# One batch projected ahead of layer 0's attention, the other three beneath its first groups

## The reference, cut to what matters

```
x = x + attn0(layernorm(x))      # 16 heads of 8, causal, softmax(q k^T / sqrt(128)) v, then Wo
x = x + moe(layernorm(x))        # 8 experts, top 2, silu(gate) * up, down
x = x + attn1(layernorm(x))      # rms norm, 16 query heads over 4 key heads, no mask, rotary factor
x = x + ffn1(layernorm(x))       # 128 -> 512, a sine transform, relu, 512 -> 128
```

## Time and profile before

| | us |
|---|---|
| median of 3 runs | 1916.95 (1916.47 to 1917.86) |
| profiled execution | 1903.78, its span 1901.6 |
| TensorE busy | 1729.3 |
| VectorE busy | 1371.3 |
| ScalarE busy | 1132.7 |
| GpSimd busy | 307.9 |

### The profile page before, as it was taken

How to read it: one execution, slowest core, us unless ns; L and a number is a source line. 1 busy time by engine, 2 the same in 40 slices (tenths; PEclk the granted TensorE clock), 3 DMA queues, 4 the chain that set the end, 5 groups by cost and what they waited for, 6 DMA issues and landing times.

```text
span 1901.6 us, 30821 instructions
## 1 busy us (share of the span) xinstructions
PE 1729.3 (91%) x10574; PEld 711.1 (37%) x10574; DVE 1371.3 (72%) x2373; ACT 1132.7 (60%) x2396; POOL 307.9 (16%) x407
## 2 busy tenths in 40 slices
PE   4599999998888989999789999999999999999876
PEld 2234444443444346666322222222222222222354
DVE  5577777777778536455787888888888888883386
ACT  2236666665555654333323777777777777777776
POOL 4100000001222225545610000000000000000265
PEclk9779999999999999999656999999999999999998
DMA  7644545333220102131331111111111111000000
GB/s 205 165 95 109 130 127 132 67 46 42 46 41 14 28 23 57 54 90 43 100 77 18 18 18 18 18 18 18 18 18 18 18 18 18 1 2 1 1 23 23
DMA packets 97576, 93.73 MB, mean 49 GB/s; under 512 B 47214, under 2 KB 75507, under 8 KB 95376
## 3 DMA queue, kind: packets, MB, share of 16 engines
q1 hardware_dynamic: 79872, 48.01, 15.3%
q0 software_dynamic: 9920, 37.87, 5.6%
q10 hardware_dynamic: 7632, 5.88, 1.1%
HBM read 48.03 MB, written 40.86 MB: 47 GB/s over the span
## 4 chain that ended last, share of the span: by engine, by line
PE 70%; DVE 14%; ACT 5%; issue 4%; POOL 3%; DMA 3%; ACTq 1%; POOLq 0%; DVEq 0%; SPq 0%
PE ps L855 20%; PE ps L839 17%; PE ps L806 17%; DVE rowmax L1488 8%; PE ps L1035 2%; PE ps L1015 2%; ACT probs L1228 2%; DMA k_parts<-Q 2%; PE ps L1007 2%; PE ps L871 2%; PE ps L1025 2%; ACTq L1145 1%; PE ps L809 1%; PE ps L842 1%; ACT oT L1232 1%
## 5 line engine op out<-in xcount | busy, mean ns | idle before, releaser
L1488 DVE TENSOR_REDUCE rowmax<-ps 128x1 f32<-128x1024 f32 (+7 forms) x1024 | 974.5, 987 | 249.2 <-PE ps L806 125.1
L1228 ACT ACTIVATE probs<-ps 128x512 f32<-128x512 f32 (+3 forms) x1792 | 859.6, 556 | 365.7 <-PE ps L839 225.5
L806 PE MATMUL ps<-K,Q 72*128 72x512 bf16 (+3 forms) x1792 | 541.0, 376 | 41.6 <-DVE rowmax L1488 32.3
L839 PE MATMUL ps<-Q,K 75*128 75x512 bf16 (+3 forms) x1792 | 537.3, 361 | 14.0 <-ACT probs L1228 9.8
L855 PE MATMUL ps<-probs,V 128*9 128x512 f32 (+3 forms) x3584 | 442.2, 555 | 0.0
L839 PEld LDWEIGHTS ps<-Q,K 75*128 75x128 bf16 x1792 | 166.0, 98 | 371.5 <-ACT probs L1228 269.5
L806 PEld LDWEIGHTS ps<-K,Q 72*128 72x128 bf16 x1792 | 151.4, 99 | 338.3 <-DVE rowmax L1488 182.5
L585 POOL TENSOR_SCALAR rtmp<-mv 128x4 f32<-128x4 f32 x8 | 1.9, 234 | 808.3 <-DVE mv L1407 808.3
L809 PE MATMUL ps<-causal,identb 128*128 128x128 bf16 x512 | 115.7, 228 | 0.0
L855 PEld LDWEIGHTS ps<-probs,V 128*9 128x9 f32 x3584 | 60.5, 89 | 144.4 <-ACT probs L1228 77.8
L1736 DVE TENSOR_TENSOR Q<-ps,Q 128x352 f32<-128x352 f32 x78 | 40.9, 524 | 98.5 <-ACT Q L1275 84.6
(11 more groups left out here) (227 smaller groups left out, 1421.5 us busy)
## 6 DMA issues: line engine op xcount, KB each, us to landing
dispatch<-wg POOLq DMA_DIRECT2D x16, 1170.0 KB, 9.0
Q<-q_parts SPq DMA_DIRECT2D x288, 64.0 KB
K<-k_parts SPq DMA_DIRECT2D x144, 64.0 KB
q_parts<-Q POOLq DMA_DIRECT2D x16, 384.0 KB, 3.6
Q<-dispatch SPq DMA_DIRECT2D x78, 65.0 KB, 1.8
probs<-returned SPq DMA_DIRECT2D x8, 512.0 KB, 4.0
k_parts<-Q POOLq DMA_DIRECT2D x8, 384.0 KB, 8.0
V<-v SPq DMA_DIRECT2D x16, 144.0 KB
```

What stands on the lines that cost most here:

```text
L806: last = pe.matmul(buf[:, c:e], Q[0:CROSS, slot, j, i * P:(i + 1) * P], K[0:CROSS, slot, kj, c:e], start=True, stop=not diag)
L839: last = pe.matmul(ps[:, bank, c:HALF], K[0:KROWS, q, kj, t * P:(t + 1) * P], Q[0:KROWS, q, j, h * HALF + c:(h + 1) * HALF], start=True, s ...
L1228: act.activation(probs[:, (4 * m + j) % PR, c:HALF], ps[:, B_BANKS[(4 * m + j) % 3], c:HALF], ACT.Exp, scale=SCALE).then_inc(sl["exp_done" ...
L1488: dve.tensor_reduce(rowmax[:, par, 8 * j + i:8 * j + i + 1], score_a(i % 2)[:, 0:hd.keys(i)], AX, ALU.max).then_inc(sl["max_done"], 1)
```

## The change

Layer 0's `project` now does blocks 0 and 1 only. Blocks 2 to 7 are done by `project_later`, whose steps hang on a events of groups 0 to 4 (`STARTS`), in banks 1 and 3, with their parts in a piece of `attn` that is free until group 8. Statistics are taken batch by batch (`STATS`); POOL inverts batch 0's before its later constants, the others ahead of the blocks' writes. SyncE issues the 20 weight loads instead of ScalarE, behind load(0,1) and ahead of load(0,2), and each `load(b, q)` of layer 0 waits for its own batch's blocks only. In layer 1 `probs` has 16 buffers; the second eight lie in wg and wu, which nothing reads by then. Both strings of `ORDERS` are others. The fills of the dispatch buffers wait for later groups. Of `project_later` there is one on TensorE, ScalarE and VectorE each, in this order below; on ScalarE H copies hT, VT copies V, Q0 and K0 are the high parts (Q0 after the parts of the block before are written), Q1 and K1 the middle ones; on VectorE QR and KR are the rests, Q2 and K2 the low parts.

```diff
-PR = 8
+PR = (8, 16)
 ORDERS = [
-    "bbbbaabpaabbbabapabbbabbpbbbabapcabbbatbpnbababbabbapapaabbababbababbapbbbaabpbampsabbabbabbbappactn",
-    "bbbbababbpbabbapbbababbpbabbabpbbababbpabbapbbababbpbbbapcabbtnbpbabbabbapbabbabbapabbbabpbbbababpmsbbbabapbabbbapapactn",
+    "bbbaabbabapababbabbbappabbababbabbabapbcabbabpbabababtppbnababbabbabbappababbababbabbpbmasbbbappcatn",
+    "bbbbaabbpbabbabbbabbabpbabbabpbababbpbbaabbpbbababpbbababpbabbabpcbababpbabbabpbababbpabbbtpnmsbbbaabbpbabbapbbbaappactn",
 ]
+FIRST = 2
+STARTS = {2: at(1, 0), 3: at(3, 0), 4: at(6, 0), 5: at(9, 0), 6: at(12, 0), 7: at(15, 0)}
+STATS = {1: at(0, 0), 2: at(4, 0), 3: at(10, 0)}
+LATER = {
+    "tensor": steps({}, [("T", at(0, 1)), ("V", at(0, 3)), ("Q", at(1, 1)), ("K", at(1, 1))], STARTS),
+    "scalar": steps({}, [("H", at(0, 2)), ("VT", at(0, 4)), ("Q0", at(1, 2)), ("K0", at(1, 2)), ("Q1", at(1, 4)), ("K1", at(1, 5))],
+                    STARTS),
+    "vector": steps(steps({}, [("SA", 0), ("SB", 2), ("SC", 3)], STATS),
+                    [("N", 0), ("QR", at(1, 2)), ("KR", at(1, 3)), ("Q2", at(1, 5)), ("K2", at(1, 6))], STARTS),
+}
...
                 def load(b, q):
+                    if l == 0:
+                        sp.wait_ge(sl["v_taken"], 2 * b + 2 + AT_ONE)
+                        for half in range(2):
+                            sp.wait_ge(sl["parts_written"][half], 32 * (b + 1))
...
                 for q in range(2):
                     load(0, q)
-                sp.wait_ge(sl["v_taken"], NG + AT_ONE)
-                for half in range(2):
-                    sp.wait_ge(sl["parts_written"][half], 32 * (NG // 2))
+                if l == 0:
+                    for dst, source in weights:
+                        sp.dma_start(dst, source).then_inc(w_in, 16)
+                else:
...
                 load(0, 2)
                 negmax_rows(0, 0)
...
-                    pool.wait_ge(s[0]["attn_done"], (g * fills + c) * 7 // 8 + 1 + AT_ONE)
+                    pool.wait_ge(s[0]["attn_done"], 8 + (g * fills + c) // 2 + AT_ONE)
...
+            def project_later(step):
+                sl = s[0]
+                for kind, u in LATER["tensor"].get(step, ()):
+                    pe.wait_ge(sl["max_done"], 32 + 8 + step - 1)
+                    if kind == "T":
+                        pe.wait_ge(sl["normed"], u + 1)
+                        turn(tokens, 1, sl["turned"])
+                    elif kind == "V":
+                        pe.wait_ge(sl["h_ready"], u + 1)
...
+                    elif kind == "Q":
+                        pe.matmul(ps[:, 1, :], wqvk[:, 0:D], hT[:, :], start=True, stop=True).then_inc(sl["q_out"], 1)
+                    else:
+                        pe.matmul(ps[:, 3, :], wqvk[:, 2 * D:3 * D], hT[:, :], start=True, stop=True).then_inc(sl["k_out"], 1)
...
-            for dst, src in weights:
-                act.dma_start(dst, src).then_inc(w_in, 16)
...
+            def project_later(step):
+                    if kind == "H":
+                        act.wait_ge(sl["turned"], u + 1)
+                        act.activation(hT[:, :], ps[:, 1, :], ACT.Copy).then_inc(sl["h_ready"], 1)
...
+                                if j == 0 and (l == 0 or G * g + m >= PR[1] // 4):
+                                    act.wait_ge(sl["pv_done"], G * g + m + 3 - PR[l] // 4)
...
+            def project_later(step):
+                    if kind[0] == "S":
+                        statistics_of_batch(u, "ABC".index(kind[1]))
+                    elif kind == "N":
+                        dve.wait_ge(sl["rstd_ready"], u // 2 + AT_ONE)
+                        dve.wait_ge(sl["turned"], u)
...
+                    elif kind in ("QR", "KR"):
+                        dve.wait_ge(sl["hi_done"], 2 * u + n + 1)
+                        dve.tensor_tensor(rest_later[:, n, :], ps[:, 1 + 2 * n, :], parts_later[:, n, 0, :], ALU.subtract)\
+                            .then_inc(sl["rest_done"], 1)
+                    else:
+                        dve.wait_ge(sl["mid_done"], 2 * u + n + 1)
...
```

More of the change, by code:

```diff
@@ L514, in _ @@
                     load(0, q)
-                sp.wait_ge(sl["v_taken"], NG + AT_ONE)
-                for half in range(2):
-                    sp.wait_ge(sl["parts_written"][half], 32 * (NG // 2))
+                if l == 0:
+                    for dst, source in weights:
+                        sp.dma_start(dst, source).then_inc(w_in, 16)
+                else:
+                    sp.wait_ge(sl["v_taken"], NG + AT_ONE)
+                    for half in range(2):
+                        sp.wait_ge(sl["parts_written"][half], 32 * (NG // 2))
                 load(0, 2)
@@ L552, in _, with inverse_of_batch @@
             own = Chain(pool, pool_own, own_wait=True)
+            def inverse_of_batch(b):
+                pool.wait_ge(s[0]["stats_ready"], b + 1)
+                apart(pool)
+                tiles = slice(b * BT, (b + 1) * BT)
+                own.done(pool.tensor_scalar(rtmp_b[:, tiles], mv_all[:, tiles, 1], LN_EPS, 1.0, ALU.add, ALU.mult))
+                own.done(pool.tensor_tensor(rstd_all[:, tiles], rtmp_b[:, tiles], power_b[:, :], ALU.pow))
+                pool.sem_inc(rstd_first if b == 0 else s[0]["rstd_ready"], 1)
             own.done(pool.memset(ident[:, :], 0.0))
@@ L565, in _ @@
             pool.wait_ge(consts, 4)
+            inverse_of_batch(0)
+            own.done(pool.memset(ones_rows(0, 2), TWO_ONES))
+            pool.sem_inc(k_ones, 1)
             apart(pool)
@@ L628, in scatter_tile @@
                                         bounds_check=2 * B * S - 1, oob_is_err=False).then_inc(tile_out[k], 16)
-            def inverse_of_batches():
-                for b in range(B):
-                    pool.wait_ge(s[0]["stats_ready"], b + 1)
-                    apart(pool)
-                    tiles = slice(b * BT, (b + 1) * BT)
-                    own.done(pool.tensor_scalar(rtmp_b[:, tiles], mv_all[:, tiles, 1], LN_EPS, 1.0, ALU.add, ALU.mult))
-                    own.done(pool.tensor_tensor(rstd_all[:, tiles], rtmp_b[:, tiles], power_b[:, :], ALU.pow))
-                    pool.sem_inc(rstd_first if b == 0 else s[0]["rstd_ready"], 1)
             def inverse_rms(u):
@@ L778, in project @@
                 projected(0, 0)
+                if l == 0:
+                    projected(1, 1)
+                    return
                 for half in range(2):
@@ L960, in route @@
                     if kind == "WO":
+                        pe.wait_ge(w_in, 16 * len(weights))
                         pe.wait_ge(pre["copied"], TURNS["T1", u] + 1)
@@ L1415, in normalise, with statistics_of_batch @@
                 last.then_inc(done, 1)
-            def project(l):
-                sl = s[l]
-                rows = (P, P if l == 0 else KV * HD)
-                def statistics_of_batch(b):
+            def statistics_of_batch(b, piece):
+                half = BT // 2
+                if piece < 2:
                     dve.wait_ge(x_in[b], 16)
                     apart(dve)
-                    for k in range(BT):
+                    for k in range(piece * half, (piece + 1) * half):
                         last = dve.bn_stats(stats_b[:, k, :], x[:, b * BT + k, :])
                     own.done(last)
+                else:
                     apart(dve)
@@ L1467, in project @@
                 if l == 0:
-                    for b in range(B):
-                        statistics_of_batch(b)
+                    for piece in range(3):
+                        statistics_of_batch(0, piece)
                 norm(0)
@@ L1472, in project @@
                 if l == 0:
-                    dve.wait_ge(sl["rstd_ready"], B - 1 + AT_ONE)
+                    for half in range(2):
+                        body(half, half, False)
+                    return
                 for v in range(NG // 2 - 1):
@@ L1504, in normalise_out @@
                 def normalise_out(g, b, q, h, bank):
+                    if l == 0 and g == 8 and h == 0:
+                        for half in range(2):
+                            dve.wait_ge(sl["parts_written"][half], 32 * (NG // 2))
                     dve.wait_ge(sl["o_turned"], 2 * g + h + 1 + AT_ONE)
```

100 lines of the change are left out of this document (81 added, 19 removed).

## The result

Before: 1917.4 us, median (1916.47 to 1919.89). After: 1955.26 us (1944.46 to 1958.81). The ratio is 1.0192 [1.0168, 1.0216]: the change makes the kernel 37.9 us slower, and the forecast of 1915, with its range to 1935, was wrong. The profiled execution of after took 1958.81 us, 1.8 more than its span.

The account below looks back on a forecast made before the run. Both attentions were taken as bound by TensorE's own instructions. The terms -9.4 + 19.8 + 7.8 + 0.7 + 0.5 - 12 - 9.6 gave -2.2 us, so about 1915 us, range 1896 to 1935.

Parts of the forecast that it names:

- the one for stalls: Groups 0 to 4: stalls from VectorE's waits and added work, 1.3 us a block beside TensorE's 3.3, +7.8 us with statistics apart.
- part 2: Layer 0's attention: six blocks beneath groups 0 to 4, costing +19.8, +7.8, +0.7 and +0.5 us.
- TensorE's work: Groups 0 to 4: six blocks' TensorE instructions all go on the path, 6 x 3.3 = +19.8 us.
- Rival C: Groups 0 to 4: VectorE's wait for ScalarE's high part costs more, whole time 1931 to 1936 us; chance 0.21.
- The start: Ahead of group 0's exponentials: their start moves from 115.9 to about 106.5 us, set by SP's queue, -9.4 us.
- rival B: Ahead of group 0: the weights go beneath the Q and K loads, whole time 1904 us; chance 0.16.
- The orders: Attention groups: new orders save 0.75 us a group in layer 0 (-12) and 0.6 in layer 1 (-9.6).
- Statistics and load(1,0): Groups 0 to 4: three batches' statistics on VectorE +0.7 us; load(1,0) waiting for blocks 2 and 3 +0.5 us.
- the fills': Groups 4 to 7: four dispatch buffer fills a group cost nothing; otherwise the row is late by up to 5 us.

Follow-up runs that it names:

- e5: e4 with TensorE's instructions of the six blocks run a second time in groups 0 to 4, results unread, nobody waiting; 1925.27 us.
- e6: e5 plus ScalarE's copies and VectorE's normalisations, subtractions and statistics of the blocks on their own data, no waits between engines; 1939.27 us.
- e3: The changed kernel with SyncE's weight loads issued behind the first row of negated maxima; 1933.52 us.
- e10: e3 with each block's normalisation four steps earlier on VectorE; 1922.88 us.
- the second one: The kernel before, unchanged, profiled once more; that execution took 1910.74 us.
- e9: e4 with the early start, all eight blocks before attention, own parts buffers, weights on POOL's queue, group 0's row ahead of load(0,2); 1887.75 us.
- e4: The kernel before with both new orders and layer 1's 16 probs buffers, projection and weights as before; 1905.52 us.
- e7: e3 with three windows per block and K taken one window after Q; 1965.81 us.
- e11: The changed kernel with the weights issued by ScalarE on its own queue from 54 us on, instead of SP; 1955.23 us.

## Why the prediction was wrong

**The step that failed** is the one for stalls in part 2: "I take 1.3: +7.8." TensorE's work was right (19.8 forecast, 19.0 in e5). What comes on top of it isn't 7.8 but 33.1 us, 5.5 a block (30.0 by the medians): 14.3 by the other engines' added work and 18.8 by the handoffs, the clock in both. Rival C had the sign and the place, with its threshold of 2.3 us a block; but even its whole price of a routed group, 8.0 a block with TensorE's part, is less than the 8.7 measured. Three things were wrong in the working:

- The lower value was taken because TensorE's own 3.3 us were to "give VectorE time to catch up". e6, where the block's pieces wait for nothing, contradicts it: 14.3 us are lost there all the same.
- The stall was looked for on VectorE, with row maxima behind its wait for ScalarE's high part. In the trace of after waits for row maxima are only 2.2 us, and VectorE itself waits only 1.2 us for high parts. TensorE waits at the block's own instructions, 7.5 us for tokens and 1.5 for hT, and at the next score matmul for a bank that the block used, 5.5 us until VectorE has taken the rests and 2.2 until ScalarE has copied v. TensorE, VectorE and ScalarE, each working in order, meet here several times a block. The routed group from which the bound came has other handoffs.
- The price of a stall was counted as its length. In after against e6 the same instructions took 6.9 us more busy time at the lower granted clock, and in e3 against e10 8.8.

**The start**: -4.1 instead of -9.4 against the forecast's own execution, and +3.0 against the second one; the mechanism was right, the size off, and the gain it was counted on isn't shown to exist. The row landed at 111.6 instead of 106.2. hT came at 16.1, not 14.2, loads at 32.3, not 30.4, so 2 us were late from the outset, and the first load ended at 53.1, not 49.0; the weights and load(0,2) took the rest. TensorE stood idle from 84, as forecast, and rival B (weights beneath the loads) didn't come true; e3 shows that the row's place in the queue is worth 23 us. "SP's issuing isn't the limit, at 0.3 to 0.5 us each" was wrong for the weights: issuing them held SP for up to 8.96 us, and in before's own chain of waits ScalarE's issues of them reach 5.61 us.

The 2 us at the outset are in the timeline above. VectorE's four pieces of the first normalisation take 4.23 us instead of 1.11, and end 0.66 us after POOL's fill of K, which by the trace started 0.07 us later than they did; the first piece alone took 3.66. In e9, where that fill is over by 7.7, they take 1.11 again. The Trainium skill (SBUF — State Buffer, Who interferes with whom) says that VectorE in a two-port mode and GpSimd compete for the same ports, that whoever issues first has them for the whole instruction, and that the other one blocks. The trace agrees that one engine was held until the other was done; that VectorE was in such a mode isn't shown, and it was the one held although the trace lists its piece as the earlier.

**The orders**: layer 0's plain groups -1.33 instead of -0.75, layer 1's -0.21 instead of -0.6. In layer 1 the busy time of a group did fall by 0.61, from 47.09 to 46.48, as forecast; but the idle time rose from 0.56 to 0.96, which the forecast had not looked for. The waits named in that group are 0.3 us for the exps and 0.3 for the output's copy, as before, and 0.3 more before the turn of the negated maxima. The routed groups, a lower end of 0 in the forecast, brought 1.5 in all in after and 4.1 in e4, since the new order lengthens some of them.

**Statistics and load(1,0)**, forecast at 0.7 and 0.5: neither has a wait of its own in after. The statistics are part of e6's 14.3. The load's margin was thin, and so was the fills', as e7 shows.

**What stays open.** How the last 18.8 us divide between waits, clock and POOL's part by cause, since a wait brings idle time and a lower clock both; why two or three routed groups run at a lower clock with the new order of layer 0; what varies in the experts' stage between 361 and 386 us and in the start's transfers between 7.5 and 11.8 us; and whether the row was late by its place in the ring or by the bytes in flight, which e11 didn't tell apart.

## What to carry to other kernels

Work that is moved beneath a stage bound by one engine costs that engine's time, then what it delays on the other engines, then every meeting of the engines, and the clock that goes with the idle gaps: here 3.2, 2.4 and 3.1 us a block, the last two less surely divided than added up. Price it by adding the instructions engine by engine with nothing waiting, as in e5 and e6, before building the handoffs. And first ask why the stage that is to be emptied is long: here the parts had two buffers for eight blocks, and the cure for that, with the earlier start and the row ahead (e9), brought 14.8 us beside the orders, where the move was to bring 9.4 at the start and pay for it in the groups.

A small transfer on which the next stage hangs goes ahead of the large ones in its queue, and clear of bursts on the others: behind four fills on POOL's queue the row of e7 came 14.4 us late. An engine that issues large loads may itself be held for tens of microseconds.

## What the runs showed of the hardware

Issuing isn't always 0.3 to 0.5 us: SP was held 7.92 us by the issue of wo and 8.96 by that of wu behind two loads of 18 Q and K transfers each, and ScalarE 34.45 us by three loads of wd while SP's loads ran. VectorE's normalisation took 3.1 us more beside a fill on POOL. ScalarE's table load, which before came at 26.70 behind its weight issues, went to 1.34 once these were gone and cost nothing. And two profiled executions of one kernel can lie 16 us apart in one stage with nearly the same busy times, and 7 us apart in another; a second profile of before would have shown that at once.
